# Leftover rows of two experts in one job: 36 routed jobs in place of 39

## What is computed

```python
x = layernorm(x)                                   # T = 2048 tokens, D = 512
scores = softmax(x @ gate_w)                       # E = 8 experts
topk_w, topk_idx = top_k(scores, 2)                # each token chooses two: 4096 choices
g = silu(x @ w_gate[e]) * (x @ w_up[e])            # H = 352
routed = sum over chosen e of topk_w * (g @ w_down[e])
shared = (silu(x @ sw_gate) * (x @ sw_up)) @ sw_down
out = x_in + routed + shared
```

## Time and profile before

| | us |
|---|---|
| median of 3 runs (lowest, highest) | 674.31 (672.37, 676.15) |
| the profiled execution: its time / its span | 676.39 / 674.3 |
| PE busy, share of the span | 646.2, 96% |
| DVE / ACT / POOL busy | 411.5 / 267.8 / 190.4 |
| start of the first routed gate product / last scatter issued | 425.3 / 664.9 |

### The profile page before, as it was taken

The page is one execution under the profiler, slowest core; times in us unless marked ns, Lnnn a source line. Parts: engine busy times, 40 slices in busy tenths (PEclk is TensorE's granted clock), DMA queues, the critical chain, the costliest instruction groups (busy, mean ns, idle before and its releaser), DMA issues.

```text
span 674.3 us, 11781 instructions
## 1 busy us (share of the span) xinstructions
PE 646.2 (96%) x3787; PEld 425.8 (63%) x3788; DVE 411.5 (61%) x770; ACT 267.8 (40%) x407; POOL 190.4 (28%) x246
## 2 busy tenths in 40 slices
PE   8999999999999999999999999999999999999991
PEld 7777677677776756665665656666556666666650
DVE  5998987988998756677677676333333323333330
ACT  4463643554442435466757764211111111111110
POOL 5210230231103334111211211244344444444321
PEclk9999999999999999999999999999999999999995
DMA  7741014413426697586886332578989887779742
GB/s 229 284 152 32 16 51 124 139 48 76 135 72 195 189 216 205 138 186 164 182 181 163 51 69 48 110 116 139 134 140 123 138 134 134 135 132 138 132 62 40
DMA packets 110836, 86.89 MB, mean 129 GB/s; under 512 B 79728, under 2 KB 85872, under 8 KB 110800
## 3 DMA queue, kind: packets, MB, share of 16 engines
q1 hardware_dynamic: 88848, 43.94, 28.9%
q0 software_dynamic: 12736, 29.50, 25.3%
q10 hardware_dynamic: 9216, 12.98, 6.2%
HBM read 44.45 MB, written 23.33 MB: 101 GB/s over the span
## 4 chain that ended last, share of the span: by engine, by line
PE 54%; DMA 13%; DVE 5%; issue 3%; SPq 1%; POOL 0%; ACT 0%; POOLq 0%; ACTq 0%; DVEq 0%
PE ps_y L565 15%; PE ps_g L565 13%; PE ps_u L565 13%; DMA out_dram<-y_job,job_tok 9%; PE ring L408 8%; PE turn_h L585 2%; DMA x_in<-x_job 2%; DMA x_job<-xn_scratch,job_tok 1%; PE ps_norm L425 1%; SPq L802 1%; DMA xg_odd<-xn_hl 1%; DVE routed L1506 1%; DMA out_dram<-x 1%; DVE den L1381 0%; PE ps_den L489 0%
## 5 line engine op out<-in xcount | busy, mean ns | idle before, releaser
L1167 ACT CAST hidT<-turn_h 128x384 f16<-128x384 f32 x71 | 33.9, 478 | 173.1 <-PE turn_h L585 167.3
L1022 POOL DMA_INDIRECT out_dram<-y_job,job_tok x39 | 61.7, 1583 | 99.8 <-DVE y_job L1789 51.8
L565 PE MATMUL ps_y<-routed,hidT 128*128 x351 | 83.3, 383 | 1.3 <-DVE hidT L1442 1.3
L565 PE MATMUL ps_g<-routed,x_in 128*128 x468 | 82.6, 313 | 1.6 <-DMA x_in<-x_job 1.6
L408 PE MATMUL ring<-xnT_h,wq_h 128*128 128x512 f32 x188 | 76.6, 408 | 2.7 <-DVE wq_l L1325 1.4
L565 PE MATMUL ps_u<-routed,x_in 128*128 x468 | 76.2, 312 | 0.0
L1449 DVE SCALAR_TENSOR_TENSOR hid<-ps_u,job_hid,silu 128x352 f32<-128x352 f32 x39 | 22.8, 584 | 85.6 <-PE ps_u L565 76.7
L408 PE MATMUL ring<-xnT_h,wq_l 128*128 128x512 f32 x188 | 74.4, 396 | 0.0
L408 PE MATMUL ring<-xnT_l,wq_h 128*128 128x512 f32 x188 | 74.1, 394 | 0.0
L565 PE MATMUL ps_y<-shared,hidT 128*128 128x512 f16 x288 | 67.4, 379 | 1.5 <-DVE hidT L1442 1.4
L565 PE MATMUL ps_g<-shared,x_in 128*128 128x352 f16 x384 | 67.4, 313 | 0.0
(11 more groups left out here) (253 smaller groups left out, 1078.9 us busy)
## 6 DMA issues: line engine op xcount, KB each, us to landing
x_res<-in_L_attn_x_dram SPq DMA_DIRECT2D x20, 256.0 KB, 3.4
routed<-in_L_ffn_w_gate_dram ACTq DMA_DIRECT2D x6, 704.0 KB, 4.8
routed<-in_L_ffn_w_up_dram ACTq DMA_DIRECT2D x6, 704.0 KB, 6.6
out_dram<-x SPq DMA_DIRECT2D x16, 256.0 KB, 3.5
xn_scratch<-xn_hl SPq DMA_DIRECT2D x16, 256.0 KB, 2.6
out_dram<-y_job POOLq DMA_DIRECT2D x16, 256.0 KB
x_in<-in_L_attn_x_dram SPq DMA_DIRECT2D x12, 256.0 KB, 3.4
routed<-in_L_ffn_w_down_dram ACTq DMA_DIRECT2D x6, 512.0 KB, 8.0
```

Of the source, the lines that this page charges most:

```text
L565: ins = pe.matmul(ps, a[i][:, k, :], w(j, k), start=(start and q == 0), stop=(stop and q == len(steps) - 1))
L1022: pool.indirect_dma_start(out[:, :], bass.IndirectOffsetOnAxis(job_tok[:, r:r + 1], 0), y_job[:, b, :], None, compute_op=ALU.add).then_inc ...
L1167: act.copy(hidT[:, 0], turn_h[:, 0:FC, :]).then_inc(s["hidTh_s"], 1)
```

## The change

Each expert's choices are cut into whole jobs of 128 rows and, where 1 to 64 rows are left, one half job of 64 rows; 65 or more rows left take a whole job. That bounds the number of jobs by 36. Four of the 36, numbers 8, 9, 26 and 27, are pairs: their lower 64 rows belong to one expert and the upper 64 to another. In a pair each step of a product is two matmuls of 64 columns of the token side, at array columns 0 and 64, each with its own expert's weights, into the lower and the upper 64 partitions of the same PSUM tile.

The lower expert's weights are read where they lie. Those of the upper expert are first copied within SBUF, over the shared expert's weights (dead by then; room for two), by three DMAs per expert on SP's queue: one behind each transpose of r = 2 to 7 (for pairs 8 and 9) and of r = 12 to 17 (for 26 and 27). PE waits for the copy (`copied`) before a pair.

A pair's rows go to the output in two indirect DMAs of 64 rows, the second issued when the first has landed. The routing on VectorE gets further small operations, in `first_slots` 6, in `slots` 11 (3 on 128 x 128 elements, 8 on 128 x 32), in `job_experts` one more comparison and reduction over 320 elements and some small ones, in `tables` 1. POOL prepares seven more constants. SP's loop over jobs is written out, and PE's loop is cut into three with the pairs written out between them.

```diff
+    HALF = P // 2
+    JOBS = ((TOPK * T + E * (HALF - 1)) // HALF + 1) // 2
+    PAIRS = E // 2
+    SIDE = JOBS // 2
+    PAIR_AT = 8
+    FIRST_PAIRS = (PAIR_AT, SIDE + PAIR_AT)
+    is_pair = lambda r: r % SIDE in (PAIR_AT, PAIR_AT + 1)
...
+        copy_raw = shared[:, :].rearrange("p (e n) -> p e n", n=EXPERT)
+        copy_done = shared[:, :].bitcast(F16).rearrange("p (e n) -> p e n", n=2 * EXPERT)
...
+            def pair_product(ps, a, ws, n, inside=None):
+                steps = [(i, j, k) for k in range(n) for i, j in ((0, 0), (0, 1), (1, 0))]
+                for q, (i, j, k) in enumerate(steps):
+                    if q == 3 and inside is not None:
+                        inside()
+                    for h in range(2):
+                        rows = slice(HALF * h, HALF * (h + 1))
+                        ins = pe.matmul(ps[rows, :], a[i][:, k, rows], ws[h](j, k), start=(q == 0),
+                                        stop=(q == len(steps) - 1), tile_position=(0, HALF * h))
+                return ins
...
+            def routed_pair(r):
+                pe.wait_ge(s["copied"], 16 * 3 * (pair_of(r) + 1))
+                return list(zip(routed_unit(r), expert_parts(copy_done, pair_of(r) % HALVES)))
...
+            after_pairs = 0
+            for pair in FIRST_PAIRS:
+                with pe.Fori(after_pairs // 2, pair // 2 - 1) as i:
+                    job_step(2 * i, 0)
+                    job_step(2 * i + 1, 1)
+                job_step(pair - 2, 0)
+                job_step(pair - 1, 1, next_pair=True)
+                job_step(pair, 0, pair=True, next_pair=True)
+                job_step(pair + 1, 1, pair=True)
+                after_pairs = pair + 2
...
+            def copy_expert(d, i):
+                if i == 0 and d < HALVES:
+                    sp.wait_ge(s["y_s"], NT)
+                    sp.wait_ge(s["split_s"], len(pieces))
+                elif i == 0:
+                    sp.wait_ge(s["y_s"], NT + FIRST_PAIRS[0] + d - HALVES + 1)
+                e = sp.value_load(job_e[0:1, JW + d:JW + d + 1], min_val=0, max_val=E - 1)
+                part = slice(*(GATE_AT, UP_AT, DOWN_AT, EXPERT)[i:i + 2])
+                sp.dma_start(copy_raw[:, d % HALVES, part],
+                             routed[:, 0:E * EXPERT].rearrange("p (e n) -> p e n", n=EXPERT)[:, e, part])\
+                    .then_inc(s["copied"], 16)
...
+            COPY_FROM = (2, FIRST_PAIRS[0] + 4)
+            for r in range(JOBS):
+                turn_gathered(r)
+                for side in range(2):
+                    if 0 <= r - COPY_FROM[side] < 6:
+                        copy_expert(2 * side + (r - COPY_FROM[side]) // 3, (r - COPY_FROM[side]) % 3)
...
+                pool.indirect_dma_start(out[:, :], bass.IndirectOffsetOnAxis(job_tok[0:HALF, r:r + 1], 0),
+                                        y_job[0:HALF, b, :], None, compute_op=ALU.add).then_inc(s["yo_half"], 16)
+                pool.wait_ge(s["yo_half"], 16 * (pair_of(r) + 1))
+                pool.indirect_dma_start(out[:, :], bass.IndirectOffsetOnAxis(upper_tok[0:HALF, pair_of(r):pair_of(r) + 1], 0),
+                                        y_job[HALF:P, b, :], None, compute_op=ALU.add).then_inc(s[f"yo{b}"], 16)
...
+                link(dve.tensor_tensor(tab_a[:, :, :], slot_e[:, :, :], per_t(whole_end), ALU.is_ge))
+                link(dve.tensor_tensor(tab_a[:, :, :], tab_a[:, :, :], per_t(left_by), ALU.mult))
+                link(dve.tensor_tensor(slot_e[:, :, :], slot_e[:, :, :], tab_a[:, :, :], ALU.add))
...
+                for least, by in ((PAIR_AT, 2), (SIDE + PAIR_AT, 2), (JOBS + 2, SIDE - 2), (JOBS, PAIR_AT - JOBS)):
+                    link(dve.tensor_scalar(slot_by[:, :], slot_j[:, :], float(least), float(by), ALU.is_ge, ALU.mult))
+                    link(dve.tensor_tensor(slot_j[:, :], slot_j[:, :], slot_by[:, :], ALU.add))
```

More of the change, by code:

```diff
@@ L44, in preln_decay_attention_moe @@
     TOPK = 2
-    JOBS = (TOPK * T - E) // P + E
-    JOBS -= 1 if (TOPK * T + E * (P - 1)) // P < JOBS else 0
-    JW = JOBS + JOBS % 2
+    HALF = P // 2
[4 more added lines that the diff above has]
+    FIRST_PAIRS = (PAIR_AT, SIDE + PAIR_AT)
+    assert JOBS == 36 and PAIRS == 4
+    is_pair = lambda r: r % SIDE in (PAIR_AT, PAIR_AT + 1)
+    pair_of = lambda r: 2 * (r // SIDE) + r % SIDE - PAIR_AT
+    JW = JOBS
+    JE = JW + PAIRS
     ROWS = T + P
@@ L567, in product, with gate_pair, up_pair, down_pair @@
                 return ins
+            def pair_product(ps, a, ws, n, inside=None):
[8 more added lines that the diff above has]
+                return ins
+            def gate_pair(u, t, tb, ws, inside=None):
+                pe.wait_ge(s[f"xin{tb}"], 8 * (t - tb) + 16)
+                pe.wait_ge(s["silu_s"], u)
+                pair_product(ps_g[:, 0:F], x_halves(tb), ws, KC, inside).then_inc(s["g_mm"], 1)
+            def up_pair(u, tb, ws):
+                pe.wait_ge(s["hid_s"], u)
+                pair_product(ps_u[:, 0:F], x_halves(tb), ws, KC).then_inc(s["u_mm"], 1)
+            def down_pair(u, t, ws):
+                pe.wait_ge(s["hidT_s"], u + 1)
+                pe.wait_ge(s["y_s"], t)
+                pair_product(ps_y[:, :], [hidT[:, h] for h in range(2)], ws, FC).then_inc(s["y_mm"], 1)
             def gate_product(u, t, tb, w, first=False, inside=None):
@@ L747, in _, with job_step @@
                     gate(last + 1)
[L749 removed]
+            def job_step(r, b, ahead=2, pair=False, next_pair=False):
                 u = HALVES * NT + r
[L752 to L760 removed]
+                t = NT + r
+                if ahead == 0:
+                    turn_hidden(u)
+                elif next_pair:
+                    gate_w, up_w = routed_pair(r + 1)[0:2]
+                    gate_pair(u + 1, t + 1, 1 - b, gate_w, inside=lambda: turn_hidden(u))
+                    up_pair(u + 1, 1 - b, up_w)
+                else:
+                    gate_w, up_w = routed_unit(r + 1)[0:2]
+                    gate_product(u + 1, t + 1, 1 - b, gate_w, inside=lambda: turn_hidden(u))
+                    if ahead == 2:
+                        up_product(u + 1, 1 - b, up_w)
+                if pair:
+                    down_pair(u, t, routed_pair(r)[2])
+                else:
+                    down_product(u, t, routed_unit(r)[2], True, True)
                 if ahead == 1:
@@ L894, in _ @@
                 turn_tile(t)
[L895 to L902, removed]
+            COPY_FROM = (2, FIRST_PAIRS[0] + 4)
[4 more added lines that the diff above has]
+                        copy_expert(2 * side + (r - COPY_FROM[side]) // 3, (r - COPY_FROM[side]) % 3)
+            sp.wait_ge(s["yo_half"], 16 * PAIRS)
             for q in range(2):
```

123 lines of the change are left out of this document (83 added, 40 removed).

## The result

The changed kernel takes 683.28 us (679.79 to 687.36, 5 runs) where the kernel before took 673.01 (672.21 to 676.15, 5 runs) beside it. The ratio is 1.0167, 95% interval 1.014 to 1.0195, so it is 11.2 us slower by the ratio (10.3 by the medians) where no change was forecast. That kernel was run again beside each group of experiments (medians 675.55, 672.79, 673.26 and 674.50 us), so kernels of different groups are compared by their ratios, which leave out runs more than 1.5% above the shortest of their kernel. The profiled execution after took 682.16 us, its span 680.3.

A forecast was written before the change was run, and what follows sets the result against it. PE was taken to set the pace, with no slack for gathers and transposes up to 530 us. Terms -17.5 + 3.0 + 3.4 + 7 + 2.5 + 1.5 = -0.1 gave a median of 674.2 us, range 662 to 688.

The forecast's parts named there:

- Two scatters in place of one: POOL's scatters of pairs: a pair adds 4.05 us, mostly covered by POOL's idle; 2.5 us at first pairs, 1.5 at tail.
- Three jobs fewer: PE's chain in the job stage: three jobs of 5.85 us go away, 17.5 us saved.
- the changes between full and half array: PE at the pairs: ten changes in and out of the half array at 0.3 us, 3 us (2 to 7).
- the routing: VectorE's added small operations, partly hidden beside PE in units 5 to 7: 3.4 us on PE's chain (2.5 to 4).
- the waits in front: Sign in the profile after: PE idle before `ps_y` in units 5 to 7, 3 us in sum.
- The copies: DMA engines in the job stage: copies only partly fit beside other traffic, ending in PE's waits; 7 us (0 to 26).
- PE's waits for `x_in`: Sign in the profile after: `ps_g` waits 5 to 10 us in sum, jobs 3 to 17, DMA share near 1.
- Halves in sequence: Rival on PE: a pair's halves don't run beside each other, 5.5 us more a pair, 696 us; chance 0.12.
- Copies fit: Rival in the job stage: copies fit and half scatters hide, 663.2 us, up to 669; chance 0.27.
- Copies add in large part: Rival in SP's queue and DMA engines: copies delay transposes or gathers PE waits for, 680 to 693 us; chance 0.17.

The follow-up runs named there:

- without copies: Changed kernel with a scatter waiting only for one of another expert, twelve copies and their wait left out: 663.92 us, ratio 0.9847 to the kernel before.
- the last one: Changed kernel, scatters waiting by expert, copies on ACT's queue, second side's copies moved behind jobs 14, 16, 18, 19, 21, 23: 663.88 us, ratio 0.9829.
- two destinations: Changed kernel with odd jobs adding to a scratch tensor, so a scatter waits only for the one of two jobs before: 670.96 us, ratio 0.9958.
- the last two runs: Changed kernel, scatters waiting by expert, copies on ACT's queue: 669.93 us; the same with the second side's copies moved to later, spread jobs: 663.88 us.
- twelve runs of one kernel: Changed kernel with scatters waiting by expert and copies on ACT's queue, second side's in consecutive jobs: 669.93 us, ratio 0.9951.

## Why the prediction was wrong

**The step that failed is "Two scatters in place of one"**, 2.5 us at the first pairs and 1.5 at the tail, 4.0 in the sum. The run with one scatter a pair measures 14.7. The half scatter itself was priced nearly right: 4.05 us with its gap was taken, and the eight starts were followed by the next after 3.97 to 4.66 us, 4.43 on average. The path was named too ("POOL holds the next gather meanwhile"), and it is the one that PE's waits show. Wrong was the slack that was set against the cost. I let POOL's 2.78 us of idle at 551.52 cover most of a second scatter. But an idle POOL is not an idle chain: while POOL waits for `y_job`, the scatter before is still in flight, and the row names only what came last. Rows of the kernel before that I had not weighed, from POOL's timeline and then from the chain that ended last:

```profile
545.86 1.59 POOL L1022 DMA_INDIRECT out_dram<-y_job,job_tok  x1 [1.57 <-DVE y_job L1789]
```

```profile
463.53 4.63 DMA out_dram<-y_job,job_tok
...
634.75 4.88 DMA out_dram<-y_job,job_tok
640.42 4.95 DMA out_dram<-y_job,job_tok
647.10 6.30 DMA out_dram<-y_job,job_tok
```

On that chain a scatter took 4.6 to 6.3 us beside other work, not the 4.38 of the very last one, which ran alone. At 4.9 (an estimate from these) the one from 545.86 landed at 550.8; with 0.7 from landing to the next issue, as in the chain after, the next could start at 551.5, and it did at 551.52. By this estimate the chain had next to nothing to spare where I counted 2.78. Worked with that, a pair adds 2 x 4.43 - 5.7 = 3.2 us that nobody gives back; four are 12.6, and the tail stands on top. The 683 lies within the range of 662 to 688 all the same, but by luck: that range was wide for the copies and for the rivals, not for this term.

**Three jobs fewer, the changes between full and half array, and the routing** came out near their prices, as far as periods show it. The trace with neither copies nor second scatters has the outputs around the first pairs 6.23, 6.36, 5.96 and 6.07 us apart in place of 5.85 each: 1.2 us a side, 2.4 in all, where 3.0 was taken. Of the routing, the down products after, which answer to the earlier trace rows:

```profile
275.89 2.12 PE L589 MATMUL ps_y<-shared,hidT 128*128 128x512 f16 x9 [0.48 <-DVE hidT L1544]
...
283.51 2.12 PE L589 MATMUL ps_y<-shared,hidT 128*128 128x512 f16 x9 [1.30 <-DVE hidT L1544]
...
290.35 2.12 PE L589 MATMUL ps_y<-shared,hidT 128*128 128x512 f16 x9 [0.52 <-DVE hidT L1544]
```

Units 6 and 7 are 7.62 and 6.84 us long where the earlier trace rows have 6.14 and 6.15: 1.5 and 0.7 longer, beside 1.9 and 0.8 in the sum. Unit 5 is 0.6 longer (6.50 in place of 5.88), so 2.8 in all, and the waits in front, 2.3 us in sum, are those that were to be looked for. -17.5 + 2.4 + 2.8 is -12.3, and the two kernels in which neither series nor copies cost much, without copies and the last one, lie at -10.3 and -11.5.

**The copies** were priced at 7 and measured 5.3: the size held, the reason did not. They do not fail to fit; 224 GB/s went through on the first side, and 250 on the second with one scatter for a pair, with PE at 36.00 of 36. PE's waits for `x_in`, 5 to 10 us foreseen, were 12.6, but 11.7 of that stand without the copies and 4.1 with one scatter for a pair: they belong to the scatters in the main. By the windows the copies cost 1.05 to 1.8 us on the first side where they stand ahead of transposes in SP's queue (4.3 with two destinations) and none on ACT's; the rest falls on the second side beside late scatters, as far as windows tell. Of the 16 DMA engines' time the four copies took some 24.6 us, near the 26 taken (an estimate: a queue share of 9.8% with them on ACT's queue, 6.1% without them, of a span of 663.7 us). The sum with the measured terms, -12.3 + 5.3 + 14.7, is +7.7; the measured +11.2 is 3.5 more. The run with neither lacks as much (-8.2 in place of -12.3), and the 3.4 us by which its last outputs come late are of that size; what makes them late, beyond the series, I can't place.

**The rivals.** Halves in sequence: refuted by the pair's rows. The Trainium skill (TensorEngine Tiling (Array Packing), "Restrictions and Gotchas") says that column tiling excludes the fast weight load. A load of 64 columns did take 110 ns where one of 128 takes 98, but two lie side by side in a step of 149, so the rule has no price here. Copies fit: true for the first side in the last two runs and for the second in the run with one scatter for a pair, not in the kernel as changed. Copies add in large part (680 to 693): its band held the result, its mechanism was not the cause.

## What to carry to other kernels

A chain of transfers that must land one after the other is an engine of its own: take its period from start to start and its slack from landing to next issue, not from the idle time of the engine that issues it. Where it is level with the busiest engine, fewer units of work gain nothing if the chain keeps its number of links (39 scatters before, 40 after). Look also at what stands behind the chain in the issuing engine's order (here the gathers): more output buffers did not help while that order stayed; asking which neighbours really conflict did. A bulk transfer ahead of a latency-critical one in its queue is worth moving, but here only PE's waits show it, and the time of that run alone did not.

## What the runs showed of the hardware that was not expected

On the chain that ended last in the changed kernel a scatter of 64 rows took 3.6 to 3.8 us and one of 128 rows 4.6 to 7.5, most of them 4.6 to 5.1: half the rows took much more than half the time. In series, scatters of the same jobs (15 to 22) took 4.8 to 5.1 us in the changed kernel and 5.3 to 5.8 in the one without copies; what decides that stays open. So does why twelve runs of one kernel spread from 665.61 to 673.91 us.

PE's last down product follows a wait of 1.26 us in every kernel. It took 2.11 us in nine of the fourteen traces and 3.1 to 3.8 in the other five; the granted clock was 1.00 in the one of the nine and 0.55 in the one of the five that stand above. What decides it stays open.

The Trainium skill (DMA: Bandwidth & Descriptors, "Rules for kernel authors") says that spreading transfers over issuing engines does not help bandwidth and saves only issue time. For bandwidth the trace agrees, 221 GB/s from SP's queue and 223 from ACT's. Yet the 1.05 us of idle time that PE had in that window was gone, so the choice of queue did matter for what stands behind the copies.
